# A selective-scan unit and the end of a pair: half a projection, gelu and silu are reordered, and VectorE takes over three steps at the end

## The chip, the cores and the metric

The kernel runs on one core of a Trainium2 chip. The metric is the device time of one execution in microseconds. The engines are named as in the profile: PE (TensorE, with PEld for its weight loads), DVE (VectorE), ACT (ScalarE), POOL (GpSimd) and SP (SyncE, which issues most DMAs). Each engine runs its own list of instructions in order and waits on semaphores.

## The reference, cut to what matters

Two blocks are computed on 16 images of 48 channels and 64x64 pixels: a depthwise 3x3 conv with a routed expert (gelu, then a 1x1 "point" conv), an FFN, a frequency-domain Mamba block on four quadrants, and a second FFN. The part that the change touches is the Mamba block and the conv that runs beside it:

```python
xz = jnp.einsum('blc,ec->ble', xs, in_w)
xi, z = (xz[..., :d_inner], xz[..., d_inner:])
# 4-tap causal conv along the sequence, then
xi = jax.nn.silu(...)
delta = jax.nn.softplus(jnp.einsum('blr,dr->bld', dt, dt_w) + dt_b)
dA = jnp.exp(delta[..., None] * A)
dBu = delta[..., None] * Bm[:, :, None, :] * xi[..., None]
h = dA_t * h + dBu_t            # along the sequence of 1024
y = einsum('bds,bs->bd', h, C_t) + xi * Dp
out = einsum('bld,cd->blc', y * jax.nn.silu(z), out_w)
```

## The kernel before

The 16 images go through in 8 pairs (p). In each pair the Mamba block has 4 quadrants times 2 images, that is 8 units (v = 0 to 7), and each unit has 12 groups or slots (m = 0 to 11) of 128 rows (8 channels times 16 states) by 1024 positions. All engines walk the same written order, `scan_stage`: for every unit and slot the engine's `early(m, v+1)`, `step(v, m)`, `conv(m, v)` and `prep(m, v+1)`, in this order, each of which does something only in its own slots. So while unit v is scanned, the next unit is prepared and one eighth of the next pair's expert conv is computed. The last pair has no conv beside it.

One slot, in the lines of the profile:

- SP (`spread_delta`) copies 8 rows of delta to 128 rows by a DMA of 512 KB (arena<-dl). There are three buffers, and the DMA for group n waits until the decay of group n-3 is made.
- ACT (`decay`, L1224) makes exp(delta*A) of the group two slots ahead. It needs the DMA and a free one of three result buffers.
- PE (`broadcast_u`, L834 and L836) spreads u into two PSUM banks, one slot ahead.
- DVE multiplies it in PSUM by B (L1558) and scans (L1563).
- POOL multiplies the states by C (L1649, `product`).
- PE (`states`, L853) sums three products into y, in PSUM banks 0 and 1, in slots 4, 7 and 10 and in slot 1 of the next unit (or at the very end, for unit 7).

The next unit's preparation runs in fixed slots. PE projects the first half of xi (`project_in`, L740) in slot 11 of the unit before the one that prepares it, and the second half in slot 0. ACT makes silu of xi (L1120) in slot 1, after `step` of that slot and so behind its decay, silu of z (L1130) in slot 3, softplus and a copy of B and C (L1142, L1155) in slot 4. Each of these has a table load in front (L1209, L1180, L1136) and the exp table behind it (L977). PE's products for z (L747) and for delta, B and C (L753) stand between them. Also in slot 2 ACT copies y out of PSUM (`copy_y`, L1248), and POOL gates it with silu of z (`gate`, L1658); the next silu of z waits for that gate.

The conv: nine taps on PE (L912, slots 5 to 9), gelu on ACT (L1279, slot 10, behind that slot's decay), the point product on PE (L918, slot 11, waits for gelu), its bias on ACT (`mix_bias`, L1268, slot 0, in front of that slot's decay). The second half of xi's projection shares a PSUM bank with the conv and waits for the bias.

The end of a pair: after the last scan come POOL's last product, PE's last `states`, ACT's copy of y, POOL's gate, PE's output projection (L862, two halves), ACT's two copies out (L1238) and PE's transposes (L658) with which the inverse transform goes on. `keep_warm` (L759) gives PE four matmuls without use beside the last `states`.

## Time and profile before

| | |
|---|---|
| device time, median of 3 runs | 4347.82 us (4341.52 to 4351.54) |
| the profiled execution's own time | 4323.44 us |
| its span, first to last instruction | 4321.6 us |
| busy share of the span | PE 87%, DVE 80%, ACT 65%, POOL 55% |
| mean granted TensorE clock | 0.949 of full speed |
| chain that ended last, by engine | DVE 30%, PE 23%, issue 21%, ACT 14%, DMA 7%, POOL 5% |

The span covers the eight pairs one behind the other; about two thirds of a pair is the scan stage. The busy shares are averages over stages with different limits, so the rows further down are taken from single stages.

### The profile page before, as it was taken

How to read it: one execution, taken by the hardware profiler on the slowest of the kernel's cores; microseconds unless marked ns; L12 is line 12 of the kernel's file. 1: busy time of each engine (PE TensorE's matmuls, PEld its weight loads, DVE VectorE, ACT ScalarE, POOL GpSimd, SP SyncE). 2: the span in 40 equal slices, each digit the busy share in tenths (PEclk: the TensorE clock that was granted, in tenths of full speed). 3: DMA queues.
4: the chain of work that ended last, by engine and by line, in shares of the span. 5: the costliest groups of instructions: out<-in, count | busy, mean ns of one | idle time of the engine just before them, and what ended most of it. 6: DMA issues, size and time to landing. Idle time of an engine off the chain costs nothing.

```text
span 4321.6 us, 41656 instructions
## 1 busy us (share of the span) xinstructions
PE 3774.4 (87%) x13976; PEld 1368.9 (32%) x13976; DVE 3470.1 (80%) x3077; ACT 2792.2 (65%) x3228; POOL 2380.3 (55%) x1108
## 2 busy tenths in 40 slices
PE   6889988899879998899988999889988899878887
PEld 2332234222342223422234222432234322342223
DVE  1479977799778996699966998679976799778996
ACT  2566757677566775676666775767756677576754
POOL 0147762577426873177732787237762487525773
PEclk9999999999999999999999999999998999998878
DMA  1168861787518883288824886258861588607881
GB/s 39 45 142 206 208 153 46 182 205 197 127 55 205 205 210 88 75 203 210 202 69 108 220 205 161 75 149 204 218 152 47 142 222 199 146 15 190 196 202 44
DMA packets 186044, 644.71 MB, mean 149 GB/s; under 512 B 25660, under 2 KB 26600, under 8 KB 182280
## 3 DMA queue, kind: packets, MB, share of 16 engines
q1 hardware_dynamic: 168808, 596.95, 56.7%
q10 hardware_dynamic: 17024, 45.10, 3.5%
q8 instruction: 113, 1.85, 0.2%
q14 instruction: 99, 0.81, 0.1%
HBM read 525.40 MB, written 78.82 MB: 140 GB/s over the span
## 4 chain that ended last, share of the span: by engine, by line
DVE 30%; PE 23%; issue 21%; ACT 14%; DMA 7%; POOL 5%; SPq 0%; DVEq 0%; ACTq 0%; POOLq 0%
DVE arena L1563 12%; DVE ps L1558 11%; DMA arena<-dl 6%; PE ps L667 4%; PE ps L607 3%; PE ps L834 2%; POOL arena L1658 2%; PE ps L658 2%; POOL arena L1649 2%; ACT arena L1020 2%; ACT arena L1224 2%; ACT arena L1002 2%; PE ps L853 2%; PE ps L686 1%; PE ps L740 1%
## 5 line engine op out<-in xcount | busy, mean ns | idle before, releaser
L1649 POOL TENSOR_TENSOR arena<-arena 128x1024 f32<-128x1024 f32 x768 | 1804.4, 2358 | 737.6 <-DVE arena L1563 737.6
L1563 DVE TENSOR_TENSOR_SCAN arena<-arena,ps 128x1024 f32<-128x1024 f32 x768 | 1756.4, 2287 | 75.2 <-issue 35.7
L1224 ACT ACTIVATE arena<-arena,a_all 128x1024 f32<-128x1024 f32 x768 | 869.4, 1146 | 798.1 <-DMA arena<-dl 656.1
L1558 DVE TENSOR_TENSOR ps<-ps,arena 128x1024 f32<-128x1024 f32 x768 | 929.5, 1210 | 116.1 <-PE ps L836 115.6
L834 PE MATMUL ps<-arena,spread 32*128 32x512 f32 x1536 | 890.9, 661 | 137.3 <-DVE arena L1563 136.3
L836 PE MATMUL ps<-arena,spread 32*128 32x512 f32 x1536 | 883.7, 663 | 0.0
L853 PE MATMUL ps<-arena,gather 128*32 128x512 f32 x3072 | 533.1, 643 | 18.8 <-POOL arena L1649 18.8
L912 PE MATMUL ps<-x 96*96 96x512 f32 x1008 | 500.3, 614 | 23.8 <-ACT arena L1155 23.8
L834 PEld LDWEIGHTS ps<-arena,spread 32*128 32x128 f32 x1536 | 232.8, 188 | 779.1 <-DVE arena L1563 411.9
L1608 POOL TENSOR_TENSOR x<-x,arena 96x512 f32<-96x512 f32 x64 | 113.3, 1771 | 373.0 <-DVE arena L1402 373.0
L977 ACT ACT_TABLE_LOAD x226 | 290.0, 1283 | 24.7 <-DMA wo<-in_wo 20.6
L740 PE MATMUL ps<-arena,w_in 96*96 96x512 f32 x512 | 258.3, 634 | 0.1
L912 PEld LDWEIGHTS ps<-x 96*96 96x96 f32 x1008 | 142.9, 163 | 348.5 <-issue 348.5
L607 PE MATMUL ps<-arena,average 96*96 96x512 f32 x400 | 226.3, 649 | 29.9 <-ACT arena L1013 29.6
L853 PEld LDWEIGHTS ps<-arena,gather 128*32 128x32 f32 x3072 | 106.5, 114 | 403.9 <-issue 300.8
L1002 ACT ACTIVATE arena<-ps,eps 96x512 f32<-96x512 f32 x200 | 136.8, 684 | 148.5 <-PE ps L607 148.2
L836 PEld LDWEIGHTS ps<-arena,spread 32*128 32x128 f32 x1536 | 229.5, 188 | 0.0
L1658 POOL TENSOR_TENSOR arena<-arena 96x1024 f32<-96x1024 f32 x64 | 150.5, 2352 | 134.3 <-ACT arena L1248 134.3
L1627 POOL MEMSET arena<- 96x6 f32 x8 | 0.8, 103 | 399.5 <-DVE xq L1525 399.5
L1371 DVE TENSOR_TENSOR arena<-ps,arena 96x512 fp8e5<-96x512 f32 x128 | 86.9, 679 | 129.3 <-ACT arena L1007 129.1
L1020 ACT ACTIVATE arena<-ps 128x1536 f16<-128x1536 f32 x128 | 183.8, 1436 | 1.7 <-PE ps L626 1.6
L1608 POOL TENSOR_TENSOR x<-col_all,arena 96x512 f32<-96x512 f32 x64 | 104.3, 1629 | 144.4 <-DVE arena L1402 144.4
(157 smaller groups left out, 4896.1 us busy)
## 6 DMA issues: line engine op xcount, KB each, us to landing
arena<-dl SPq DMA_DIRECT2D x880, 512.0 KB, 6.9
dl<-arena ACTq DMA_DIRECT2D x64, 384.0 KB, 5.7
x<-pn SPq DMA_DIRECT2D x56, 247.5 KB, 10.2
arena<-in_x SPq DMA_DIRECT2D x9, 1536.0 KB, 16.2
arena<-xq SPq DMA_DIRECT2D x64, 192.0 KB, 6.1
arena<-arena ACTq DMA_DIRECT2D x64, 192.0 KB, 7.5
out<-x SPq DMA_DIRECT2D x64, 192.0 KB, 2.1
arena<-xq SPq DMA_DIRECT2D x64, 191.8 KB, 5.4
```

The lines of the kernel that those rows point to most:

```text
L607: pe.matmul(ps[0:R, LN_DEPTH + j % LN_DEPTH, :], average[:], sq[:, j % LN_DEPTH, :], start=True, stop=True).then_inc(averaged, 1)
L740: mm = pe.matmul(ps[0:DI, 6 + c, :], w_in[:, q, j, :], xs[:, i, c * 512 + 2 * j:c * 512 + 2 * j + 512], start=(j == 0), stop=(j == 1))
L834: pe.matmul(ps[:, bank, :], spread[rows[0], r, :], u[rows[0], i, 0:512], start=True, stop=True)
L836: pe.matmul(ps[:, bank + 1, :], spread[rows[1], r, :], u_low[rows[1], i, :], start=True, stop=True).then_inc(ubc_ready, 1)
L853: mm = pe.matmul(ps[b * BLK:(b + 1) * BLK, c, :], gather[:, r, :], hs[:, (r * TRIO + b) % HSS, c * 512:(c + 1) * 512], start=False, stop=( ...
L912: mm = pe.matmul(ps[0:R, 7, :], diag[:, k, :], taps_of(win[:, v % 2], k), start=(k == 0), stop=(k == TAPS - 1), skip_group_check=True)
L977: exp_table = lambda: act.preload_act_table_set("natural_log_exp_and_others")
L1020: act.activation(hf[:, j % 2, :], ps[:, 4:7, :].rearrange("p b n -> p (b n)"), ACT.Copy).then_inc(hf_ready, 1)
L1224: act.activation(da[:, m % DAS, :], dbc[:, m % DBC, :], ACT.Exp, scale=a_all[:, v // 2, m:m + 1]).then_inc(da_ready, 1)
L1558: dve.tensor_tensor(driven, driven, bmat[:, v % 2, :], ALU.mult).then_inc(bu_ready, 1)
L1563: dve.tensor_tensor_scan(hs[:, m % HSS, :], da[:, m % DAS, :], driven, 0.0, ALU.mult, ALU.add).then_inc(h_ready, 1)
L1649: pool.tensor_tensor(product, product, cmat[:, v % 2, :], ALU.mult).then_inc(pr_ready, 1)
```

## The change

Four things are moved or rewritten.

1. PE: the first half of xi's projection for the unit after next (slot 11) is issued in front of the point product instead of behind it (`half_ahead`).
2. ACT: gelu is issued in front of slot 10's decay instead of behind it, and silu of xi in front of slot 1's decay instead of behind it.
3. The end of a pair: DVE makes the last product, the gate (straight from PSUM, so that no copy of y is made) and the second half of the copy out. POOL and ACT no longer do these.
4. `keep_warm` at the end of a pair has three matmuls instead of four, and one more stands in each of slots 0, 2 and 4 of unit 7.

```diff
-WARM_XI, WARM_SCAN, WARM_GATE = 4, 2, 4
+WARM_XI, WARM_SCAN, WARM_GATE = 4, 2, 3
+WARM_LAST = {0: 1, 2: 1, 4: 1}
...
-                    if slot == PE_XI_EARLY and v + 1 < UNITS:
-                        pe.wait_ge(xs_in[1 - i], (p * QUADS + (v + 1) // 2 + 1) * XSL)
-                        pe.wait_ge(bc_ready, bc_count(p, v))
-                        if v >= 3 and i == 1:
-                            pe.wait_ge(mo_copied, 2 * (p * QUADS + (v - 1) // 2))
-                        project_in(V + 1, (v + 1) // 2, 1 - i, 0)
...
                 def states(v, r):
-                    pe.wait_ge(pr_ready, (p * UNITS + v) * G + TRIO * (r + 1))
+                    if v == UNITS - 1 and r == GPB - 1:
+                        pe.wait_ge(last_pr, p + 1)
+                        pe.wait_ge(pr_ready, pr_count(p, v, G - 1))
+                    else:
+                        pe.wait_ge(pr_ready, pr_count(p, v, TRIO * (r + 1)))
...
+                def half_ahead(v):
+                    q, i = divmod(v + 2, 2)
+                    pe.wait_ge(xs_in[i], (p * QUADS + q + 1) * XSL)
+                    pe.wait_ge(bc_ready, bc_count(p, v + 1))
+                    if v >= 2 and i == 0:
+                        pe.wait_ge(mo_copied, 2 * (p * QUADS + v // 2))
+                    project_in(p * UNITS + v + 2, q, i, 0)
...
                 def conv(slot, v):
                     if v == UNITS - 1:
                         invert_early(slot)
+                        keep_warm(WARM_LAST.get(slot, 0))
+                    if slot == PE_XI_EARLY and v + 2 < UNITS:
+                        half_ahead(v)
...
                 def early(slot, v):
+                    if slot == ACT_SILU and v >= 2:
+                        act.preload_act_table(ACT.Silu)
+                        silu_xi(v)
+                        exp_table()
...
                 def prep(slot, v):
-                    if slot == ACT_SILU and v >= 2:
-                        act.preload_act_table(ACT.Silu)
-                        silu_xi(v)
-                        exp_table()
...
                 def step(v, m):
+                    if m == ACT_GELU and not last:
+                        gelu(v)
...
                 def final():
-                    copy_y(UNITS - 1)
...
-                    copy_out(QUADS - 1, 1, 7)
...
+                def final():
+                    dve.wait_ge(h_ready, n + 1)
+                    dve.tensor_tensor(hs[:, slot, :], hs[:, slot, :], cmat[:, i, :],
+                                      ALU.mult).then_inc(last_pr, 1)
+                    dve.wait_ge(y_acc, (V + 1) * GPB)
+                    dve.wait_ge(sz_ready, 2 * V + 2)
+                    dve.wait_ge(mo_ready, 2 * (p * QUADS + q))
+                    dve.tensor_tensor(yz[:, i, :], two(0, DI), sz[:, i, :], ALU.mult).then_inc(yz_ready, 1)
+                    dve.wait_ge(mo_ready, 2 * (p * QUADS + q) + 2)
+                    dve.tensor_copy(colq[:, q // 2, q % 2][:, QH // 2:QH, :],
+                                    ps[:, 7, :].rearrange("p (h w) -> p h w", w=QH)).then_inc(mo_copied, 1)
...
                 def step(v, m):
+                    if v < UNITS - 1 or m < G - 1:
+                        pool.tensor_tensor(product, product, cmat[:, v % 2, :],
+                                           ALU.mult).then_inc(pr_ready, 1)
...
                 def final():
-                    gate(UNITS - 1)
```

The order of instructions on ACT around the border of two units, from the decay of the next unit's group 0 to copy_y, before. L1224 is a decay, L1275 and L1279 are gelu's table and gelu, L977 is the exp table, L1268 the conv's bias, L1209 and L1120 silu's table and silu of xi, L1248 copy_y.

```order
L1224 ACTIVATE arena<-arena,a_all 128x1024 x3
L1275 ACT_TABLE_LOAD
L1279 ACTIVATE arena<-ps,sel_small 96x512
L977 ACT_TABLE_LOAD
L1224 ACTIVATE arena<-arena,a_all 128x1024
L1268 ACTIVATE x<-ps,pw_bias 96x512
L1224 ACTIVATE arena<-arena,a_all 128x1024 x2
L1209 ACT_TABLE_LOAD
L1120 ACTIVATE arena<-ps,small_all 96x512 x2
L977 ACT_TABLE_LOAD
L1248 ACTIVATE arena<-ps 96x1024
```

The same place on ACT in the changed kernel, where the lines have moved: L1240 is a decay, L1290 and L1294 are gelu, L993 the exp table, L1286 the bias, L1196 and L1136 silu of xi, L1264 copy_y.

```order
L1240 ACTIVATE arena<-arena,a_all 128x1024 x2
L1290 ACT_TABLE_LOAD
L1294 ACTIVATE arena<-ps,sel_small 96x512
L993 ACT_TABLE_LOAD
L1240 ACTIVATE arena<-arena,a_all 128x1024 x2
L1286 ACTIVATE x<-ps,pw_bias 96x512
L1240 ACTIVATE arena<-arena,a_all 128x1024
L1196 ACT_TABLE_LOAD
L1136 ACTIVATE arena<-ps,small_all 96x512 x2
L993 ACT_TABLE_LOAD
L1240 ACTIVATE arena<-arena,a_all 128x1024
L1264 ACTIVATE arena<-ps 96x1024
```

One decay (group 0) has moved from ahead of gelu to behind it, and one (group 3) from ahead of silu of xi to behind it.

PE in slots 10 and 11 of the unit before, and in slot 0: L834 and L836 are a broadcast, L918 is the point product, L740 a half of xi's projection.

```order
L834 MATMUL ps<-arena,spread 128x512
L836 MATMUL ps<-arena,spread 128x512
L918 MATMUL ps<-arena,pw_gated 96x512
L740 MATMUL ps<-arena,w_in 96x512 x2
L834 MATMUL ps<-arena,spread 128x512
L836 MATMUL ps<-arena,spread 128x512
L740 MATMUL ps<-arena,w_in 96x512 x2
```

The same place on PE in the changed kernel (L934 is the point product, L746 a half of the projection).

```order
L834 MATMUL ps<-arena,spread 128x512
L836 MATMUL ps<-arena,spread 128x512
L746 MATMUL ps<-arena,w_in 96x512 x2
L934 MATMUL ps<-arena,pw_gated 96x512
L834 MATMUL ps<-arena,spread 128x512
L836 MATMUL ps<-arena,spread 128x512
L746 MATMUL ps<-arena,w_in 96x512 x2
```

The first half of the projection and the point product have changed places.

DVE at the end of a pair, before: the last multiply (L1558) and scan (L1563), then the additions of the inverse transform (L1546) and its copies (L1473).

```order
L1558 TENSOR_TENSOR ps<-ps,arena 128x1024
L1563 SCALAR_TENSOR_TENSOR arena<-arena,ps 128x1024
L1546 TENSOR_TENSOR xd<-xd,ps 128x384 x4
L1473 COPY xq<-ps 96x8x64 x2
L1579 TENSOR_TENSOR x<-x,ps 96x512 x8
```

DVE at the end of a pair in the changed kernel (L1571, L1576, L1559 and L1486 are the lines that were L1558, L1563, L1546 and L1473).

```order
L1571 TENSOR_TENSOR ps<-ps,arena 128x1024
L1576 SCALAR_TENSOR_TENSOR arena<-arena,ps 128x1024
L1587 TENSOR_TENSOR arena<-arena 128x1024
L1592 TENSOR_TENSOR arena<-ps,arena 96x1024
L1595 COPY col_all<-ps 128x16x32
L1559 TENSOR_TENSOR xd<-xd,ps 128x384 x4
L1486 COPY xq<-ps 96x8x64 x2
```

Three rows have come in between the last scan and the additions: the last product, the gate and the second half of the copy out.

## Rows read from the trace of the kernel before

**Rows 1.** Stretches: length, busy PE, PEld, DVE, ACT, POOL, clock, DMA share, GB/s.

```profile
2414.61:2630.08 215.47, 200.44 (x700) 55.79 (x696) 204.99 (x121) 156.80 (x155) 169.78 (x76) 1.00 0.85 212
...
3974.75:4186.16 211.41, 179.22 (x600) 46.32 (x598) 205.10 (x120) 137.73 (x135) 163.82 (x71) 0.84 0.84 199
sum 1750.35, PE 1617.93 PEld 446.14 DVE 1642.39 ACT 1236.50 POOL 1353.09; mean PE 202.24 PEld 55.77 DVE 205.30 ACT 154.56 POOL 169.14
```

**Rows 2.** The page's costliest groups: busy us, mean ns, idle before it and releasers.

```profile
L1563 DVE TENSOR_TENSOR_SCAN arena<-arena,ps 128x1024 f32<-128x1024 f32 x768 | 1756.4, 2287 | 75.2 <-issue 35.7
...
L1558 DVE TENSOR_TENSOR ps<-ps,arena 128x1024 f32<-128x1024 f32 x768 | 929.5, 1210 | 116.1 <-PE ps L836 115.6
```

**Rows 3.** Timeline, pair 4, unit 2: start, length, instruction, idle before and releaser.

```profile
2437.99 1.15 ACT L1224 ACTIVATE arena<-arena,a_all 128x1024 f32<-128x1024 f32 x1 [2.29 <-DMA arena<-dl]
...
2440.19 1.15 ACT L1224 ACTIVATE arena<-arena,a_all 128x1024 f32<-128x1024 f32 x1 [1.05 <-DMA arena<-dl]
...
2441.36 1.28 ACT L1209 ACT_TABLE_LOAD   x1
...
2445.22 1.02 ACT L1248 ACTIVATE arena<-ps 96x1024 f32<-96x1024 f32 x1
...
2457.18 3.23 ACT L1224 ACTIVATE arena<-arena,a_all 128x1024 f32<-128x1024 f32 x3
...
2458.41 2.29 DVE L1563 TENSOR_TENSOR_SCAN arena<-arena,ps 128x1024 f32<-128x1024 f32 x1 [1.29 <-issue]
```

**Rows 4.** Busy time by stretch, pair 4, units 2 and 3.

```profile
2458.30:2480.60 22.30, 22.30 (x81) 6.02 (x78) 21.98 (x13) 13.58 (x15) 17.29 (x8) 1.00 1.01 263
2439.10:2458.30 19.20, 16.48 (x61) 4.67 (x60) 16.79 (x10) 17.82 (x20) 15.30 (x8) 1.00 0.69 164
```

**Rows 5.** Timeline of ACT: the first and the last of 48 decays of group 3.

```profile
309.25 1.15 ACT L1224 ACTIVATE arena<-arena,a_all 128x1024 f32<-128x1024 f32 x1 [1.04 <-DMA arena<-dl]
...
4167.90 1.15 ACT L1224 ACTIVATE arena<-arena,a_all 128x1024 f32<-128x1024 f32 x1 [1.11 <-DMA arena<-dl]
```

**Rows 6.** Timeline, pair 4, unit 1, slots 10 and 11.

```profile
2429.51 1.15 ACT L1224 ACTIVATE arena<-arena,a_all 128x1024 f32<-128x1024 f32 x1 [4.16 <-DMA arena<-dl]
...
2431.97 0.68 ACT L1279 ACTIVATE arena<-ps,sel_small 96x512 f32<-96x512 f32 x1
...
2433.65 1.88 PE L740 MATMUL ps<-arena,w_in 96*96 96x512 f32 x4
```

**Rows 7.** Three smaller groups by line, same columns as rows 2.

```profile
L759 PE MATMUL ps<-spread,gather 128*32 128x512 f32 x160 | 78.9, 635 | 11.3 <-DVE xq L1525 11.3
...
L918 PE MATMUL ps<-arena,pw_gated 96*96 96x512 f32 x112 | 62.1, 637 | 22.5 <-ACT arena L1279 22.5
...
L1538 DVE TENSOR_TENSOR arena<-arena 96x1024 f32<-96x1024 f32 x8 | 9.8, 1221 | 85.4 <-ACT arena L1142 85.4
```

**Rows 8.** Busy time by stretch: a stretch at the lower clock, pair 1, unit 4.

```profile
958.10:971.70 13.60, 13.60 (x28) 3.03 (x26) 9.55 (x6) 7.69 (x8) 6.59 (x3) 0.50 0.76 178
```

**Rows 9.** Timeline: the end of pair 4.

```profile
2691.54 2.37 POOL L1649 TENSOR_TENSOR arena<-arena 128x1024 f32<-128x1024 f32 x1 [1.09 <-DVE arena L1563]
...
2694.98 2.34 POOL L1649 TENSOR_TENSOR arena<-arena 128x1024 f32<-128x1024 f32 x1 [1.08 <-DVE arena L1563]
2697.38 0.63 PE L853 MATMUL ps<-arena,gather 128*32 128x512 f32 x3 [2.06 <-POOL arena L1649]
...
2699.35 1.02 ACT L1248 ACTIVATE arena<-ps 96x1024 f32<-96x1024 f32 x1 [6.12 <-PE ps L853]
...
2700.45 2.34 POOL L1658 TENSOR_TENSOR arena<-arena 96x1024 f32<-96x1024 f32 x1 [3.13 <-ACT arena L1248]
...
2702.85 1.94 PE L862 MATMUL ps<-arena,wo 96*64 96x512 f32 x8 [1.80 <-POOL arena L1658]
2703.97 1.91 ACT L1238 ACTIVATE col_all<-ps 128x512 f32<-128x512 f32 x2 [2.10 <-PE ps L862]
```

**Rows 10.** Busy time by stretch, sum of eight: last scan's end to the transposes.

```profile
sum 92.58, PE 53.30 PEld 12.55 DVE 0.00 ACT 34.83 POOL 46.26; mean PE 6.66 PEld 1.57 DVE 0.00 ACT 4.35 POOL 5.78
```

More of the change, by code:

```diff
@@ L404, in scan_stage, with pr_count @@
             last()
+        def pr_count(p, v, m):
+            return p * (UNITS * G - 1) + v * G + m
         def bc_count(p, v):
@@ L1268, in mix_bias, with gelu @@
                     act.activation(pwb, ps[0:R, 7, :], ACT.Identity, bias=pw_bias[:, 0:1]).then_inc(pwb_ready, 1)
[L1270 to L1281 removed]
+                def gelu(v):
+                    act.preload_act_table(ACT.Gelu)
+                    act.wait_ge(taps_ps, (p + 1) * NCH + v + 1)
+                    if v:
+                        act.wait_ge(pw_ps, (p + 1) * NCH + v)
+                    act.activation(gel, ps[0:R, 7, :], ACT.Gelu,
+                                   bias=sel_small[:, TAPS:TAPS + 1]).then_inc(gelu_ready, 1)
+                    exp_table()
                 def final():
[L1284 removed]
                     if not last:
@@ L1288, in final @@
                     copy_out(QUADS - 1, 0, 6)
-                    copy_out(QUADS - 1, 1, 7)
-                scan_stage(prep, first, step, conv, final, early)
+                scan_stage(prep, first, step, lambda slot, v: None, final, early)
                 evac_turned(p, xq, inverted, evens(NG // 2, NG), INV_BANK)
```

36 lines of the change are left out of this document (14 added, 22 removed).

## The prediction

> **What bounds the kernel now.** I read the stretches first. [rows 1] cut the scan stages: each stretch runs from the scan of group 6 in unit 1 to the same scan in unit 6, five units, and the sum is over all eight pairs. The 40 units take 1750.35 us, 43.76 each, and DVE is busy for 1642.39 of them, 41.06 each. DVE is the engine nearest to its limit, but something stops it for up to 2.7 us in each unit, 108 us in all. [rows 2] name it: 115.6 us before the multiply, ended by PE's broadcast, and 35.7 before the scan with "issue", where DVE waits for nothing that the profile names.
>
> The timeline of one unit shows what is late [rows 3]. The scan of group 6 starts at 2458.41, 1.29 late, and the decay that it needs is the first of the three that begin at 2457.18: it ends at 2458.33, so the "issue" wait is ACT. Going back from there ACT works almost without a pause to 2439.14, the end of group 2's decay: a wait of 1.05 for a DMA, group 3's decay, silu of xi with two tables (2441.36 to 2445.22), copy_y, and then the decays, silu of z and softplus that the program puts there. This chain is 19.2 us long. The broadcast that stops the multiply a step earlier hangs on the same chain: it stands on PE behind the products that wait for silu of z.
>
> What starts the chain is the landing of group 2's DMA. [rows 4] show the two halves of a cycle. From group 6's decay until the next unit's group 2 has landed (2458.3 to 2480.6) the DMA engines are full: share 1.01, 263 GB/s. While ACT's chain runs (2439.1 to 2458.3) they stand at 0.69 and 164 GB/s, and ACT is busy for 17.82 of 19.2. Full DMA, then full ACT: 22.3, a decay of 1.15 and about 19 make 42.5 a unit, which is more than DVE's 41.06. This cycle is what the scan stage runs at.
>
> Outside the scan the place to read is the end of a pair [rows 9]. From POOL's last product (2694.98) to the projection (2702.85) one engine works at a time: POOL 2.34, PE 1.95, ACT 1.02, POOL 2.34, with hops between. In the eight stretches from the last scan's end to the transposes DVE is busy for 0.00 of 92.58 us [rows 10].
>
> **Silu of xi in front of group 3's decay.** ACT now begins silu's table at the end of group 2's decay, and group 3's DMA lands while silu runs. The decay's 1.15 stays in the chain; the wait in front of it goes. That wait was 1.05 here, 1.04 in the first and 1.11 in the last of 48 places [rows 3, 5]; over the 48 its mean is 0.93. Silu also needs the second half of the projection. Taking at each of the 42 places of the first seven pairs the later of the two gives a mean of 0.87. Since the DMA half of the cycle starts at group 6's decay, it moves with the chain, and the 0.87 counts in every unit: 42 x 0.87 = 36.5 us. The DVE limit is not reached (43.1 a unit in pair 4, 41.0 busy [rows 1]). The last pair has only 211.41 - 205.10 = 6.3 to give, some of it gaps between instructions, and there the half projection comes late more often: 2.5. Sum 39; the bounds are 0, if the DMA half grows by as much, and 54 (48 x 1.05 plus a part of the PE waits). I take the upper side, because in [rows 4] the DMA engines have room exactly where group 3 is now late. What is late next: group 3's decay ends 2.8 us later than before (3.86 + 1.15 after group 2's, for 1.05 + 1.15), and DMA 6 is issued that much later. Scan 3 stands about three steps of 3.44 before the 2457.1 at which scan 6 could have gone, so it keeps 1 to 2 us, and DMA 6 lands into the slack part.
>
> **Gelu in front of group 0's decay.** ACT waits 4.16 for that decay's DMA [rows 6]; gelu's block is two tables of 1.28 and 0.68, 3.24, and fits. Where the taps end late it does not, and the decay comes up to 2.3 late; it is used some 5 us later. On ACT nothing is gained or lost: 0. If that cover were gone, 2.3 in half of 42 units, 48 us, would be the cost.
>
> **Half projection in front of the point product.** PE waited 22.5 us in all for gelu at the point product [rows 7]. The half projection (1.88 [rows 6]) now fills that time. Where there was no wait, the point product comes 1.88 later, and with it the bias on ACT, behind which group 2's decay is queued. That decay waits for its DMA anyway (2.29 [rows 3]), which covers it: 0. The PE time itself is no gain, but what follows the wait is: [rows 8] is a stretch of 13.6 us at a granted clock of 0.50, that is 1.2 GHz, right behind such a wait; DVE is busy for 9.55 in it, against 0.95 of the time in pair 4, where the clock is 1.00 [rows 1]. That is 3.4 lost. Three units (pairs 0, 1 and 3) have their chain lengthened so, by about 3 us each. I take 9 us, with bounds of -5 (it falls elsewhere) and +20.
>
> **The end of a pair.** Removed: POOL's product 2.34, copy_y 1.02, POOL's gate 2.34, and five hops of about 0.04 to 0.1 that become four: 7.87 from 2694.98, plus 0.07 before it [rows 9]. New: DVE's product at 1.22 (the nearest row with both inputs in SBUF, L1538 [rows 7]), PE's 1.95, DVE's gate from PSUM at 1.21 (L1558 [rows 2]), hops 0.1: 4.5. Gain 3.4. The three keep_warm matmuls end before that: eight rows of L759 at 0.49 [rows 7] become six. The second copy out now runs beside ACT's first, but it can start only when the projection ends at 2704.79, and ACT's pair was done at 2705.88: between 0 and 0.9, taken as 0 because a copy takes about 1 us. 8 x 3.4 = 27; bounds 18 (product at POOL's 2.34) and 34.
>
> **keep_warm in unit 7.** Three more a pair, 2 x 0.49 each, 24 us of PE. PE has no silu products to wait for in unit 7, so slots 0 and 2 are free; the one in slot 4 stands in front of taps and transforms that fill PE. It costs up to 1 a pair, and a clock that stays up gives as much back: 0, bounds -8 and +8.
>
> **Sum.** 39 + 9 + 27 = 75 us. Against the profiled execution 4323.4 - 75 = 4248. The runs shown have a median 24.4 above that execution, and the change leaves what makes that difference alone: 4347.8 - 75 = 4273 us. A change of less than 0.2% (8.7 us) can't be told from none here.
>
> **Rivals.**
> A second case is that only the end of a pair counts: the DMA half starts earlier but takes as long as it must, since the total of bytes a unit is the same, and DVE waits as before. For it speaks a DMA share of 0.85 over whole stretches [rows 1]; against it the 0.69 [rows 4]. 4347.8 - 27 = 4321.
> A third: PE's clock falls in more places, for instance in slot 3, where PE then waits for silu of z. At 3 us each, ten more of them and none saved: 4273 + 9 + 30 = 4312.
> On the other side: the point product, 1.88 later, makes the bias end after group 2's DMA has landed. From there on each microsecond delays group 2's decay and the whole chain. It decides when the bias ends later than the landing; of the 2.29 in [rows 3] the 1.88 leave 0.4. If all 42 units lost the 1.88, the scan stages would lose 42 x (1.88 - 0.87) = 42, less 27 at the ends: 4362, slower.
> A fifth: DVE's product cannot run beside POOL. If POOL still worked at the scan's end, DVE would wait up to 2.34 in each pair: 4273 + 19 = 4292. But POOL's product of group 10 ends at 2693.91, 1.0 before the last scan does, and so in all eight pairs [rows 9].
> The Trainium skill, page "SBUF — State Buffer", section "Who interferes with whom", states just this: a DVE instruction with two inputs in SBUF and a GpSimd one that reads SBUF lock each other out for the whole instruction. By that rule the new product is the first DVE instruction of the scan stage that could be held up, and the page would agree with the fifth case only if POOL were late; no run here shows such an overlap.
> A sixth: with PE no longer late the waits go further down, to DVE's limit: 108 of [rows 1] less some 12 of gaps, and 27: 4225 to 4240.
>
> **Chances.** The forecast 0.62, with a range of its own of 4255 to 4292; only the ends 0.15; more slow stretches 0.08; the bias late, slower, 0.05; POOL in the way 0.04; down to DVE's limit 0.06. The range 4240 to 4322 leaves out the slower case and the outer halves of the second and the sixth. Faster by over 0.2%: 0.92; within: 0.03; slower: 0.05.
>
> **What would show it.** In the trace after: group 3's decay without a wait, and group 6's decay 18.2 after group 2's; a mean unit near 42.8; POOL's columns of the end gone and about 7.7 from the last scan's end to the transposes; no wait of PE for gelu at the point product; fewer stretches at 0.50 at the start of a unit. The prediction is wrong if the stretch from group 6's decay to the landing of group 2 grows, if the bias on ACT waits for PE, or if DVE waits for PE at scan 3 or 5 as long as before.

## The result and the profile after

The changed kernel takes 4223.67 us (median of four runs, 4219.27 to 4236.07); the kernel before, beside it, 4344.67 (4333.06 to 4351.54). The ratio is 0.9729, with a 95% interval of 0.9699 to 0.9759: 118 us less by the ratio, 121 by the medians. The forecast was 75 less and a lowest end of 4240. The direction was right; the time lies below the range.

The profiled execution took 4219.27 us, 104 less than the one before (4323.44), at a mean granted clock of 0.967 instead of 0.949. It lies 4 us below its runs' median; the one before lay 24 below.

Stretches of the changed kernel from the scan of group 6 in unit 1 to the same scan in unit 6, cut and laid out as [rows 1]: pair 4, the last pair, the sum of eight.

```profile
2355.80:2568.98 213.18, 200.42 (x698) 55.80 (x696) 204.88 (x120) 156.34 (x155) 169.45 (x76) 1.00 0.87 213
...
3877.50:4085.62 208.12, 178.38 (x600) 46.35 (x598) 204.89 (x120) 137.43 (x135) 163.69 (x71) 0.84 0.84 202
sum 1701.78, PE 1584.70 PEld 437.74 DVE 1639.73 ACT 1234.25 POOL 1352.81; mean PE 198.09 PEld 54.72 DVE 204.97 ACT 154.28 POOL 169.10
```

The sum is 48.6 us lower and DVE's busy time the same within 3: nearly all of it is waiting that went. A unit takes 1701.78 / 40 = 42.54, where 42.8 was foreseen. PE's busy time fell by 33 for the same matmuls, most of it by a higher clock. The page's costliest groups (as [rows 2]) say which wait went:

```profile
L1576 DVE TENSOR_TENSOR_SCAN arena<-arena,ps 128x1024 f32<-128x1024 f32 x768 | 1756.4, 2287 | 74.6 <-issue 31.6
...
L1571 DVE TENSOR_TENSOR ps<-ps,arena 128x1024 f32<-128x1024 f32 x768 | 928.3, 1209 | 57.5 <-PE ps L836 57.2
```

DVE's wait for PE's broadcast halved (115.6 before); the wait behind group 6's decay is nearly as it was. The same unit as in [rows 3], in the timeline of the changed kernel:

```profile
2378.50 1.15 ACT L1240 ACTIVATE arena<-arena,a_all 128x1024 f32<-128x1024 f32 x1 [1.88 <-DMA arena<-dl]
...
2379.66 1.28 ACT L1196 ACT_TABLE_LOAD   x1
...
2383.53 1.15 ACT L1240 ACTIVATE arena<-arena,a_all 128x1024 f32<-128x1024 f32 x1
...
2396.52 3.23 ACT L1240 ACTIVATE arena<-arena,a_all 128x1024 f32<-128x1024 f32 x3
...
2397.76 2.29 DVE L1576 TENSOR_TENSOR_SCAN arena<-arena,ps 128x1024 f32<-128x1024 f32 x1 [0.64 <-DVE ps L1571]
```

Silu's table (L1196) starts 0.01 after group 2's decay, group 3's decay (2383.53) has no wait, and group 6's decay ends at 2397.67: 18.02 after group 2's, where it was 19.19. Over units 1 to 6 of the first seven pairs the mean of this chain went from 19.31 to 18.05; the time from group 6's decay to the next unit's group 2 stayed (24.62 and 24.65, 35 places). The 24.62 holds units that were slowed by half clock: in the cycles without any, this half grew by 0.3 (24.29 and 24.58). The cycle still ends at group 6.

The end of pair 4 (as [rows 9]), and the sum of the eight stretches from the last scan's end to the transposes (as [rows 10]):

```profile
2631.74 1.22 DVE L1587 TENSOR_TENSOR arena<-arena 128x1024 f32<-128x1024 f32 x1
...
2632.24 1.86 POOL L1697 TENSOR_TENSOR x<-x 96x512 f32<-96x512 f32 x1 [1.54 <-ACT x L1286]
2633.02 0.63 PE L857 MATMUL ps<-arena,gather 128*32 128x512 f32 x3 [1.64 <-DVE arena L1587]
...
2634.99 1.22 DVE L1592 TENSOR_TENSOR arena<-ps,arena 96x1024 f32<-96x1024 f32 x1 [2.03 <-PE ps L857]
...
2636.27 1.94 PE L866 MATMUL ps<-arena,wo 96*64 96x512 f32 x8 [0.44 <-DVE arena L1592]
...
2638.25 1.01 DVE L1595 COPY col_all<-ps 128x512 f32<-128x512 f32 x1 [2.04 <-PE ps L866]
```

```profile
sum 63.19, PE 40.48 PEld 10.16 DVE 27.69 ACT 18.40 POOL 11.99; mean PE 5.06 PEld 1.27 DVE 3.46 ACT 2.30 POOL 1.50
```

From the last scan's end, 2631.70, to the transposes, 2639.41, it takes 7.71; the eight sum to 63.19, 29.4 less than before. The row of POOL is the conv's last addition (`mix`); it starts while DVE's product (L1587) runs.

Between the two profiled executions the 104 us lie as follows. Units 0 to 6 of the first seven pairs make 52 of them (2138.8 and 2086.6), unit 7 of these pairs 9, the scan stage of the last pair 3, and all that stands outside the scans 40. Of the 40, 29 are the ends of the pairs, and 16 are one stage between pairs 5 and 6 that ran at half clock for 44.4 us before and does not in the changed kernel (last section). In all, the granted clock stood at half for 438 us before and for 274 after.

### The profile page after: what moved, and what is told of

Read it like the earlier page. It is cut to its first block, busy times and chain, and to the rows that moved or that the text cites. A ratio compares the mean times of both kernels' runs of the same rounds, so it can differ in the third digit from the quotient of the medians.

```text
span 4217.4 us, 41720 instructions
## 1 busy us (share of the span) xinstructions
PE 3708.7 (88%) x14008; PEld 1348.4 (32%) x14008; DVE 3493.2 (83%) x3101; ACT 2772.9 (66%) x3212; POOL 2345.8 (56%) x1092
## 4 chain that ended last, share of the span: by engine, by line
DVE 35%; issue 25%; PE 18%; ACT 13%; DMA 4%; POOL 4%; SPq 0%; DVEq 0%; ACTq 0%; POOLq 0%
DVE ps L1571 15%; DVE arena L1576 13%; PE ps L673 4%; DMA arena<-dl 3%; PE ps L613 3%; PE ps L664 2%; ACT arena L1036 2%; ACT arena L1018 2%; POOL arena L1689 2%; POOL arena L1680 2%; ACT arena L1240 2%; PE ps L692 2%; DVE arena L1424 1%; ACT L1152 1%; ACT arena L1029 1%
## 5 line engine op out<-in xcount | busy, mean ns | idle before, releaser
L1680 POOL TENSOR_TENSOR arena<-arena 128x1024 f32<-128x1024 f32 x760 | 1785.9, 2359 | 704.3 <-DVE arena L1576 704.3
L1576 DVE TENSOR_TENSOR_SCAN arena<-arena,ps 128x1024 f32<-128x1024 f32 x768 | 1756.4, 2287 | 74.6 <-issue 31.6
L1240 ACT ACTIVATE arena<-arena,a_all 128x1024 f32<-128x1024 f32 x768 | 869.8, 1146 | 692.1 <-DMA arena<-dl 541.4
L834 PE MATMUL ps<-arena,spread 32*128 32x512 f32 x1536 | 876.4, 652 | 142.7 <-DVE arena L1576 140.9
L1571 DVE TENSOR_TENSOR ps<-ps,arena 128x1024 f32<-128x1024 f32 x768 | 928.3, 1209 | 57.5 <-PE ps L836 57.2
L836 PE MATMUL ps<-arena,spread 32*128 32x512 f32 x1536 | 869.1, 653 | 0.0
L857 PE MATMUL ps<-arena,gather 128*32 128x512 f32 x3072 | 519.4, 629 | 12.5 <-DVE arena L1587 12.4
L834 PEld LDWEIGHTS ps<-arena,spread 32*128 32x128 f32 x1536 | 230.1, 186 | 785.9 <-DVE arena L1576 482.8
L746 PE MATMUL ps<-arena,w_in 96*96 96x512 f32 x512 | 246.6, 609 | 8.0 <-ACT x L1286 7.8
L857 PEld LDWEIGHTS ps<-arena,gather 128*32 128x32 f32 x3072 | 104.9, 112 | 384.8 <-issue 299.3
L836 PEld LDWEIGHTS ps<-arena,spread 32*128 32x128 f32 x1536 | 226.7, 186 | 0.0
L643 PE MATMUL ps<-arena,w 128*96 128x512 fp8e5 x384 | 105.4, 384 | 83.4 <-DVE arena L1376 77.6
```

Of the source, the lines that this page charges most:

```text
L746: mm = pe.matmul(ps[0:DI, 6 + c, :], w_in[:, q, j, :], xs[:, i, c * 512 + 2 * j:c * 512 + 2 * j + 512], start=(j == 0), stop=(j == 1))
L834: pe.matmul(ps[:, bank, :], spread[rows[0], r, :], u[rows[0], i, 0:512], start=True, stop=True)
L836: pe.matmul(ps[:, bank + 1, :], spread[rows[1], r, :], u_low[rows[1], i, :], start=True, stop=True).then_inc(ubc_ready, 1)
L857: mm = pe.matmul(ps[b * BLK:(b + 1) * BLK, c, :], gather[:, r, :], hs[:, (r * TRIO + b) % HSS, c * 512:(c + 1) * 512], start=False, stop=( ...
L1240: act.activation(da[:, m % DAS, :], dbc[:, m % DBC, :], ACT.Exp, scale=a_all[:, v // 2, m:m + 1]).then_inc(da_ready, 1)
L1571: dve.tensor_tensor(driven, driven, bmat[:, v % 2, :], ALU.mult).then_inc(bu_ready, 1)
```

## The experiments

Each kernel was compared with the kernel before on the same chip; us is (1 - ratio) x 4340. A part that is "moved" is the part of the diff shown above, alone. The intervals are some 9 to 19 us wide to either side, so differences of 20 us between two rows are at the edge of what the ratios can tell; where the text decides more finely, it goes by the traces, of which there is one for each kernel.

| kernel | ratio, 95% interval | us less | mean clock of its runs |
|---|---|---|---|
| before, again | 0.9999 (0.9969 to 1.0029) | 0 | 0.946 |
| silu of xi moved | 0.9892 (0.9847 to 0.9936) | 47 | 0.948 |
| half projection and gelu moved | 0.9983 (0.9952 to 1.0014) | 7 | 0.945 |
| end of a pair | 0.9939 (0.9907 to 0.9971) | 26 | 0.946 |
| keep_warm in unit 7 | 0.9992 (0.9970 to 1.0013) | 3 | 0.950 |
| silu, half projection and gelu | 0.9844 (0.9813 to 0.9876) | 68 | 0.960 |
| silu and gelu | 0.9845 (0.9807 to 0.9882) | 67 | 0.956 |
| silu and half projection | 0.9824 (0.9785 to 0.9862) | 76 | 0.958 |
| silu and one keep_warm in slot 11 | 0.9834 (0.9803 to 0.9864) | 72 | 0.959 |
| all but keep_warm in unit 7 | 0.9788 (0.9751 to 0.9825) | 92 | 0.960 |
| the whole change | 0.9729 (0.9699 to 0.9759) | 118 | 0.966 |

**The parts alone.** First the kernel before as a control, then three parts.

> The kernel before, unchanged, run again: a control for the step of the forecast that took the runs' offset of 24 us over the profiled execution as a constant. Theory 1 (the offset is something around the execution that stays): every execution here lies near 4345 us whatever its granted clock. Theory 2 (the offset is TensorE's clock, and the profiled execution of before was a lucky one): time and mean granted clock go together. From the two profiles 0.949 goes with 4323 us; a stretch at half clock of 13.6 us cost 3.4, a quarter, so 0.01 less clock (some 86 us more at half clock) should cost some 20 us: executions at 4345 us should show 0.935 to 0.942.

Theory 2 held in the main, with a higher clock than foreseen: executions at 4344 to 4347 us show 0.944 or 0.945. Twelve executions of one program took 4319.85 to 4363.46 us, the fastest at a clock of 0.950, the slowest at 0.940; of 28 executions of before beside them the fastest (4311.23) had 0.956. Over these 40 a fitted line loses 28 us for 0.01 of clock and accounts for some 70% of the spread. The profiled execution of before stood near the fast end.

```
-   (ACT, prep of slot 1, behind group 3's decay)  table Silu; silu_xi(v); exp_table()
+   (ACT, early of slot 1, in front of it)         table Silu; silu_xi(v); exp_table()
```

> Only silu of xi moves in front of group 3's decay. Theory 1 (the forecast's term for this edit is right, and the excess lies elsewhere): 36 to 46 us faster than before (42 units of 0.87 to 1.03, and up to 3 in the last pair), the stretches at half clock inside the scan stages remain, some 120 us of them in the first seven pairs. Theory 2 (the shorter chain on ACT is also what keeps TensorE's clock up): 65 us faster or more, and few stretches at half clock left in the scan stages. Rival (the DMA half of the cycle grows by as much): within 10 us of before.

47 us, with an interval of 28 to 66: theory 1, a little above its upper end. The traces put it lower, within the same interval. From group 2's decay to the next unit's, in units 1 to 5 of the first seven pairs, the cycles without any half clock take 43.33 and 43.27 on average in the two profiles of before (23 and 24 of 35 cycles) and 42.53 here (23): 0.77 a unit, some 32 us over 42 units, with an uncertainty of some 18.

```
-   (ACT, POOL)  copy_y(UNITS - 1); gate(UNITS - 1); copy_out(QUADS - 1, 1, 7); last product on POOL
+   (DVE)        last product; gate from PSUM; half of the copy out       WARM_GATE 4 -> 3
```

> Only the end of a pair changes: DVE makes the last product, the gate and half of the copy out, three keep_warm matmuls in place of four. Theory 1: 24 to 28 us faster (3.1 to 3.4 in each of eight pairs), nothing else moves. Theory 2 (the end also changes TensorE's clock in the stage behind it, as the 44 us stretch in pair 5 of before): 35 us or more.

26 us, with an interval of 13 to 40: theory 1 by its size. But the 44 us stretch that theory 2 speaks of is missing in this kernel's one profile, where the stage between pairs 5 and 6 takes 164.1 against 184.1 in the control: 3.4 of the 20 are the end. How often it is missing was not measured, and the ratio can't tell 27 from 27 and 16 more.

```
-   (PE)   project_in(V + 1, ..., 0) in prep of slot 11, behind the point product
+   (PE)   half_ahead(v) in conv of slot 11, in front of it
-   (ACT)  gelu in conv of slot 10      + (ACT)  gelu(v) in step of slot 10, in front of the decay
```

> Only the half projection and gelu move. Theory 1 (the forecast: they are worth the few stretches at half clock behind the wait for gelu): 0 to 10 us faster. Theory 2 (they are where the excess comes from, since they fill TensorE's wait at the border of units): 30 to 50 us faster, mean granted clock up by 0.015 or more, and nearly no stretch at half clock in slots 0 to 4 of a unit of the first seven pairs. Rival (nothing but a later bias): 0 or slower.

7 us and no more clock: theory 1 in size, but not for its reason. The stretches at half clock had not gone, they had moved: in units 0 to 6 of the first seven pairs silu alone has 95.6 us at half clock, all in slots 11 and 0, and this kernel 105.8, all but 6.8 in slots 2 and 3. The kernel before has both kinds, 54.6 and 27.3. PE's groups by line say why (columns as [rows 7]): with silu alone moved, with half projection and gelu alone, and with all three.

```profile
L747 PE MATMUL ps<-arena,w_in 96*96 96x512 f32 x256 | 124.7, 609 | 0.0
L918 PE MATMUL ps<-arena,pw_gated 96*96 96x512 f32 x112 | 63.7, 651 | 23.1 <-ACT arena L1279 22.8
```

```profile
L747 PE MATMUL ps<-arena,w_in 96*96 96x512 f32 x256 | 136.1, 657 | 29.2 <-ACT arena L1125 29.1
L923 PE MATMUL ps<-arena,pw_gated 96*96 96x512 f32 x112 | 57.7, 596 | 0.0
```

```profile
L747 PE MATMUL ps<-arena,w_in 96*96 96x512 f32 x256 | 124.7, 609 | 0.1
L923 PE MATMUL ps<-arena,pw_gated 96*96 96x512 f32 x112 | 57.7, 596 | 0.0
```

PE has two holes at the border of a unit: the point product's wait for gelu (slot 11; L918 and L923), and z's wait for silu of xi (slot 2, L747). Each edit closes one. With silu alone the first is open, and the timeline (pair 4, unit 2) shows what it costs:

```profile
2409.43 0.68 ACT L1279 ACTIVATE arena<-ps,sel_small 96x512 f32<-96x512 f32 x1
...
2410.17 1.10 PE L918 MATMUL ps<-arena,pw_gated 96*96 96x512 f32 x2 [1.73 <-ACT arena L1279]
...
2413.76 1.21 PE L834 MATMUL ps<-arena,spread 32*128 32x512 f32 x1
...
2415.89 1.23 DVE L1558 TENSOR_TENSOR ps<-ps,arena 128x1024 f32<-128x1024 f32 x1 [1.83 <-PE ps L836]
```

PE waits 1.73, its clock falls to the lower level, the broadcast takes 1.21 instead of 0.69, and DVE waits. With half projection and gelu alone the second hole opens instead, and the half clock falls on PE's products that ACT waits for (pair 6, unit 4):

```profile
3587.37 3.43 PE L753 MATMUL ps<-arena,w_dbc 96*128 96x512 f32 x4
...
3590.84 0.68 ACT L1147 ACTIVATE arena<-ps,small_all 96x512 f32<-96x512 f32 x1 [0.75 <-PE ps L753]
...
3591.90 1.23 DVE L1562 TENSOR_TENSOR ps<-ps,arena 128x1024 f32<-128x1024 f32 x1 [4.16 <-PE ps L830]
```

**The two holes together.**

> Silu of xi, gelu and the half projection move; the end of a pair and unit 7 stay as before. Alone, silu was worth 40 to 47 us and half projection with gelu 7, with the mean granted clock at 0.945 to 0.949 in each; in the first the stretches at half clock stand in slot 0 of a unit, in the second in slots 2 and 3. Theory 1 (the parts add): 47 to 54 us faster than before, clock 0.948. Theory 2 (TensorE has two holes at the border of a unit, the wait for gelu and the wait for silu of xi; each edit closes one, and the clock stays up only when both are closed): 65 to 85 us faster, mean clock 0.953 to 0.958, nearly no stretch at half clock left in slots 0 to 4 of units 1 to 6 in the first seven pairs, those in unit 7 as before.

68 us, with 47 + 7 apart, and the clock at 0.960: theory 2. Units 0 to 6 of the first seven pairs, busy time by stretch, make it plain (columns as [rows 1]). First the kernel with silu alone, which shows the price of the clock inside one execution: pair 4 at 0.94 and pair 5 at 1.00 differ by 12.5 us, and the DVE work is the same within 1.2.

```profile
2326.34:2635.89 309.55, 294.46 (x962) 81.02 (x960) 288.09 (x169) 218.02 (x215) 231.87 (x102) 0.94 0.85 207
2848.72:3145.78 297.06, 279.00 (x962) 77.48 (x960) 286.93 (x169) 217.36 (x215) 231.97 (x102) 1.00 0.88 215
...
sum 2123.02, PE 1997.73 PEld 551.50 DVE 2011.68 ACT 1523.87 POOL 1623.62; mean PE 285.39 PEld 78.79 DVE 287.38 ACT 217.70 POOL 231.95
```

The same sum of the kernel before (the control's profile), with half projection and gelu alone, and with all three:

```profile
sum 2133.86, PE 1986.04 PEld 548.67 DVE 2011.78 ACT 1527.20 POOL 1623.74; mean PE 283.72 PEld 78.38 DVE 287.40 ACT 218.17 POOL 231.96
```

```profile
sum 2145.46, PE 2004.53 PEld 555.22 DVE 2011.59 ACT 1531.06 POOL 1624.12; mean PE 286.36 PEld 79.32 DVE 287.37 ACT 218.72 POOL 232.02
```

```profile
sum 2080.86, PE 1954.57 PEld 541.98 DVE 2008.52 ACT 1521.35 POOL 1623.49; mean PE 279.22 PEld 77.43 DVE 286.93 ACT 217.34 POOL 231.93
```

In these executions silu alone gives 11, half projection and gelu alone lose 12, and together they give 53. The 12 is within the spread of one program: the same units, unchanged, take 2133.9 to 2162.2 in four profiles (before, the control, and the kernels with the end of a pair or unit 7 alone changed).

Is it the hole, or the order of the matmuls? Two kernels close it by one of the two edits:

> Silu of xi and gelu moved; the half projection stays behind the point product. Theory 2 (what counts is that TensorE has no hole in slot 11, whoever closes it): gelu comes earlier and the wait for it is gone, so clock 0.957 or more and 65 to 80 us faster than before, as with all three moved. Theory 3 (what counts is the order on TensorE: with the half projection still behind the point product, two matmuls more stand between gelu and the broadcast of group 1): 40 to 55 us faster, DVE still waits at group 1 of units 2, 4 and 6.

> Silu of xi and the half projection moved; gelu stays behind group 0's decay. Theory 2: the half projection (some 1 us) fills the wait for gelu of up to 1.7 and leaves less than 1 us of hole: clock 0.957 or more, 65 to 80 us faster. Theory 3: the same time, since the order on TensorE is the same. If gelu's place is what counts, 40 to 55 us faster and the clock at 0.948.

67 and 76 us, alike within their intervals: either will do, and theory 3 falls (DVE's waits at group 1 of units 1 to 6 are zero in the first of them). Their intervals overlap that of silu alone; what parts them from it is the clock in the profiles. In units 0 to 6 of the first seven pairs these two and the one with all three moved have 0 or 6.8 us at half clock and take 2080.9 to 2086.9. The six with a hole open (before, the control and the four with one part changed) have 64.9 to 139.9 and take 2123.0 or more. Two more fill the holes with matmuls whose result nobody uses:

```
     if slot == PE_PW:
+        keep_warm(3)
         pe.wait_ge(gelu_ready, ...)
```

> Silu of xi moved, and three keep_warm matmuls (some 1.5 us, they compute nothing that is used) in front of TensorE's wait for gelu in slot 11; half projection and gelu stay where they were. Theory 2 (the clock falls because TensorE has a hole at this place; any work that fills it keeps the clock up): mean clock 0.955 to 0.960 as with the half projection moved, 65 to 80 us faster than before, hardly a stretch at half clock in slots 0 and 11 of units 1 to 6. Rival (the moved half projection helps because what follows it comes sooner, not because the hole is filled): clock 0.948, 40 to 47 us faster as with silu alone, or less by the added work.

```
     if slot == PE_Z (v >= 2):
+        keep_warm(3)
```

> Half projection and gelu moved, and three keep_warm matmuls in front of TensorE's wait for silu of xi in slot 2 (units 2 on); silu stays where it was. Theory 2: the stretches at half clock in slots 2 and 3 of units 1 to 6 go, clock 0.953 to 0.958, and by the clock alone 25 to 45 us faster than before, where half projection and gelu alone gave 4 to 7. Rival (the hole is not what the clock goes by, or the added matmuls delay the broadcasts): within 10 us of before, clock 0.947 or less.

Both brought units 0 to 6 to a clock of 1.00 and were worth little in time: 0.9916 and 0.9990. I had sized the filler wrongly: a keep_warm shows as two matmul records of some 0.45, so three took 2.7 over a hole of 1.7, and DVE waited 0.93 or 1.90 at group 1 of most units of the first. That is not all of it: its units 0 to 6 take 2101.01, 22 less than with silu alone, and what it loses again stands in unit 7, where the filler also stands (318.3 against 308.3), and outside the scans (1541.7 against 1529.6). Why was not followed up. In the second the units 0 to 6 of seven pairs came down from 2145.46 to 2125.20, but the last pair, whose PE has no conv, lost as much to the filler (its scan stage took 359.6 instead of 340.0), and DVE still waited 83 us at groups 5 and 6 of units 1 to 6 of all pairs (97 without the filler): ACT's chain is as long as before (mean 19.05), and the clock helps little where that is late. With a filler shorter than the hole in slot 11:

> Silu of xi moved, and one keep_warm matmul in front of TensorE's wait for gelu, in place of three. The profile of the run with three shows that each is two passes of 0.45 to 0.49, so the three took 2.7 to 2.9 us over a hole of some 1.7, and DVE waited 0.93 or 1.90 at group 1 of every unit. One takes 0.9 and leaves less than 1 us of hole. Theory 2 (any work that fills the hole will do): no wait at group 1, no stretch at half clock in units 0 to 6, clock 0.956, 60 to 75 us faster than before, as with the half projection in the hole. Rival (the half projection itself has to be out of the way): 40 to 50 us faster, as with silu alone.

72 us: one matmul that computes nothing, 0.9 us in slot 11, does what moving half projection and gelu does. The sum of units 0 to 6 is between silu alone and all three:

```profile
sum 2096.45, PE 1993.30 PEld 548.74 DVE 2010.51 ACT 1522.47 POOL 1623.64; mean PE 284.76 PEld 78.39 DVE 287.22 ACT 217.50 POOL 231.95
```

**Unit 7.**

```
+WARM_LAST = {0: 1, 2: 1, 4: 1}     keep_warm(WARM_LAST.get(slot, 0)) in unit 7
```

> Only the three keep_warm matmuls in unit 7 are added. Theory 1 (the forecast's term): within 8 us of before. Theory 2 (they keep the clock up in unit 7, where before has 54 us at half clock in the first seven pairs): the stretches of unit 7 go, clock up by 0.003 to 0.006, and at some 28 us per 0.01 of clock 8 to 17 us faster.

> The changed kernel without the three keep_warm matmuls in unit 7. Theory 1 (they are worth nothing): within 8 us of the changed kernel, so 110 to 125 us faster than before. Theory 2 (they carry a part of the excess): stretches at half clock come back in slots 1 to 5 of unit 7, 40 us or more of them in the first seven pairs, clock 0.960 or less, 100 to 108 us faster than before.

Alone 3 us and undecided. Taken out of the change, 26 by the two ratios (92 and 118); the intervals overlap. The traces give less: unit 7 of the first seven pairs takes 303.7 in the change and 308.7 without them, 304.2 with them alone and 312.4 and 316.4 in the two profiles of before. So in unit 7 itself they are worth 5 to 12. In the one profile without it half clock in unit 7 is back (44.4 us there in the first seven pairs, 13.7 with it), and a stretch of 44.4 us between pairs 0 and 1, told of below, makes up 14.6 of the 27 between the two profiles. Another 10.6 lie in units 0 to 6, where the two programs are the same.

**Does ACT's chain still set the pace?** Six kernels try to beat the change. The copy of B and C, 1.02 us of the chain, goes behind group 6's decay:

```
 (ACT, early of slot 4)  softplus(v)
-                        keep_bc(v)
 (ACT, prep of slot 4)   delta_to_rows(v)
+                        keep_bc(v)
                         bc_to_rows(v)
```

> The changed kernel with the copy of B and C moved behind group 6's decay, so that ACT's chain from group 2 to group 6 is 1.02 us shorter again. Theory 1 (full DMA, then ACT's chain is still the cycle): 15 to 40 us faster than the changed kernel, group 6's decay some 17 us after group 2's. Theory 2 (after the change DVE or PE is the limit): within 8 us of it. On the other side: B and C reach PE's taps and the DMAs 1.1 later, PE gets a new hole in slot 5, and it is 5 to 20 slower than the changed kernel.

The other side came, far stronger than foreseen: ratio 1.0483, 4530 us, clock 0.894. The timeline (pair 4, unit 2) shows a third hole:

```profile
2594.47 2.82 PE L928 MATMUL ps<-x 96*96 96x512 f32 x4 [2.35 <-ACT arena L1171]
...
2597.22 1.21 PE L834 MATMUL ps<-arena,spread 32*128 32x512 f32 x1
...
2599.34 1.23 DVE L1571 TENSOR_TENSOR ps<-ps,arena 128x1024 f32<-128x1024 f32 x1 [2.19 <-PE ps L836]
```

PE waits 2.35 for the copy, then works at half clock for 14 to 17 us, in nearly every unit, and DVE waits 392.7 us in all for its broadcasts. So the hole was filled, and the taps spread in other ways (the expectations take four keep_warm for 2.0 us; in the trace they are eight records and took 3.6):

```
+WARM_TAPS = 4      keep_warm(WARM_TAPS) in front of the taps' wait in slot 5
```

> The changed kernel with the copy of B and C behind group 6's decay, as in the run that was 300 us slower than the changed kernel and showed a hole of 2.35 us on TensorE in front of the conv's taps in slot 5 and half clock behind it in most units; now with four keep_warm matmuls (2.0 us) in front of that wait. Theory 2 (all of the loss was the clock behind the hole): the stretches in slot 6 go, and the time is that of the changed kernel or up to 40 us less. Rival (the later copy of B and C costs by itself): still 50 us or more slower than the changed kernel, at a clock of 0.96.

```
-CONV_TAPS = {5: (0, 1), 6: (2, 3), 7: (4,), 8: (5, 6), 9: (7, 8)}
+CONV_TAPS = {6: (0, 1), 7: (2, 3), 8: (4, 5), 9: (6, 7, 8)}
```

> As the run before it, but the conv's taps begin in slot 6 instead of 5, so that the wait for the copy of B and C does not stand in front of the broadcasts of slot 5; the four keep_warm matmuls stay in slot 5. Theory 2: as the run before or 5 to 15 us less, and faster than the changed kernel. Rival (taps packed into four slots delay the broadcasts of slots 8 and 9, gelu comes later): 10 to 30 us slower than the changed kernel.

```
+CONV_TAPS = {6: (0, 1, 2), 7: (3, 4), 8: (5, 6), 9: (7, 8)}      WARM_TAPS = 2
```

> The changed kernel with the copy of B and C behind group 6's decay, the conv's taps from slot 6 on, three of them in slot 6 and two in each of 7 to 9, and two keep_warm matmuls in slot 5. With three taps in slot 9 DVE had waited 1.24 at group 9 in every even unit and some 0.7 in odd ones, and no longer at group 6. If that place alone took the gain back: 5 to 25 us faster than the changed kernel. If TensorE is full from slot 6 to 9 wherever the third tap stands: 20 to 50 us slower than the changed kernel, with the wait at group 7 or 8.

```
+CONV_TAPS = {6: (0, 1), 7: (2, 3), 8: (4, 5), 9: (6, 7), 10: (8,)}      WARM_TAPS = 2
```

> As the run before, but two taps in each of slots 6 to 9 and the last one in slot 10, so that gelu waits for it in front of group 0's decay. If TensorE's room in slots 6 to 9 is what was missing: 5 to 25 us faster than the changed kernel. If gelu's lateness costs (it ends behind the landing of group 0's DMA, and the point product waits for it): a hole in slot 11, half clock behind it, and 10 to 50 us slower than the changed kernel.

```
-WARM_TAPS = 4      +WARM_TAPS = 2      (taps from slot 5, as in the first of these)
```

> The changed kernel with the copy of B and C behind group 6's decay and two keep_warm matmuls in slot 5 (1.8 us for a hole of 2.35) in place of four, which took 3.6 and so kept the taps 1.3 us behind the copy that they wait for. If the overfull slot was the 1.51 that DVE waited at group 7 of every unit: no such wait, and 5 to 25 us faster than the changed kernel, 120 to 145 faster than before. If the taps are late by the copy itself: a wait of 0.5 or more at group 7, and the time of the changed kernel or slower.

Ratios 0.9916, 0.9853, 0.9784, 0.9827 and 0.9792: none beats the change's 0.9729, and each came out as the slower of the cases foreseen for it, the second slower still (54 us behind the change, where 10 to 30 stood). The half clock that was expected with the last tap in slot 10 did not come in units 0 to 6. In the last one the clock is 1.00 in units 0 to 6, the chain's mean is 17.05 and DVE's wait at group 6 is gone, but the other half of the cycle grew from 24.65 to 25.8, and DVE waits 0.7 (odd units) and 1.0 (even) on average at group 7 and 0.4 at groups 8 to 10 of even units, for broadcasts that stand on PE behind taps, keep_warm and the projection out. So in the changed kernel ACT's chain is still what is late, but with the taps in these slots shortening it gains nothing: PE's room comes right behind it.

With the last tap in slot 10 it does gain. Units 0 to 6 of that kernel, and of the change:

```profile
sum 2064.78, PE 2027.21 PEld 559.86 DVE 2011.10 ACT 1501.78 POOL 1623.47; mean PE 289.60 PEld 79.98 DVE 287.30 ACT 214.54 POOL 231.92
```

```profile
sum 2086.60, PE 1957.74 PEld 542.15 DVE 2008.72 ACT 1524.82 POOL 1624.38; mean PE 279.68 PEld 77.45 DVE 286.96 ACT 217.83 POOL 232.05
```

The 22 us are lost again in unit 7 (326.2 against 303.7), and 43 more outside the scans (1533.2 against 1489.8), where the stages behind a pair are 3 to 6 longer and one, between pairs 0 and 1, 17. A kernel with these taps in units 0 to 6 alone was not built. How much of the 24.65 is DMA and how much PE was not separated.

## Why the prediction was wrong

**The term that failed is the 9 us for PE's clock**, in the part on the half projection, together with "three units" as its extent. The mechanism was right, half clock behind a wait of PE, but not its size. The trace of before had it: in units 1 to 5 of the first seven pairs all 35 cycles take 43.99 on average, the 23 without half clock 43.33. That is 0.66 a unit, and some 28 us over 42 units (0.59 and 25 in the control). The prediction counted three stretches of 13.7 us, 41 of the 81.9 us at half clock in units 0 to 6, and left out the 27.3 that stand in slots 2 and 3, where PE waits for silu of xi. With silu moved, closing the hole in slot 11 was worth 20 to 29 us in four kernels (67 to 76 against 47, with some 20 of uncertainty); half projection and gelu without it gave 7. The prediction read one stretch [rows 8] and three units, and added the edits up. They don't add: while silu of xi is late, PE's clock falls there instead (next to the place that the third rival names, but behind silu of xi, not silu of z, and in the edit taken alone), and while gelu is late, at the other place. The parts alone sum to 47 + 7 + 26 + 3 = 83, near the forecast 75; the whole is 118, and the missing 35 have some 30 of uncertainty. 13 to 22 of them are the two holes (67 to 76 against 47 + 7); the rest lies within the intervals.

**The offset of 24 us did not stay.** "The change leaves what makes that difference alone" was wrong: a part of the difference was TensorE's clock, which varies from execution to execution, and the change takes away many of the places where it falls. By the control's line 0.949 against 0.946 makes some 10 of the 24; the rest is spread that the clock does not explain. That is 17 of the 46 us by which the forecast missed: the two profiles differ by 104, the medians by 121. Of the other 29 (104 - 75), 16 are the stage between pairs 5 and 6, which no term of the prediction touches and whose cause stays open; 9 are unit 7 and 7 are units 0 to 6. In all three it is stretches at half clock that have gone.

**Silu in front of group 3's decay: right.** 39 foreseen, 47 measured (interval 28 to 66), and by the traces some 32 in 42 units and 2 to 3 in the last pair. Group 3's decay has no wait, the chain is 1.08 shorter in the median unit (19.10 and 18.02), where 0.87 was the mean wait. The other half of the cycle grew by a quarter of that in the cycles without half clock (from 24.29 and 24.23 to 24.51 with silu alone), not by as much, so the second rival falls, for this step.

**The end of a pair: right.** 27 foreseen, 26 measured, 29 by the stretches; 7.71 from scan to transposes, where 7.7 was written. The fifth rival did not come: POOL's own products end before the last scan does. But DVE and POOL do meet, the other way round. In five of the eight pairs the conv's last addition on POOL (L1697, shown above) starts 0.5 us after DVE's product. The product takes 1.22 in all eight; the addition takes 1.84 to 1.86 in these five and 1.25 to 1.29 in its other 51 places, and ends 1.1 after the product. So POOL waited and DVE did not, and the next step of the chain, PE's sums (L857), went on without it. The Trainium skill, page "SBUF — State Buffer", section "Who interferes with whom", says that of two such instructions the order of issue decides which one is blocked. The trace agrees with that.

**Gelu at nothing, the bias covered: right.** Moved with the half projection they cost no wait that shows, and the slower rival (the bias behind the point product) did not come, though its sign did: the bias, which waited for PE once before, by 0.1, now waits in 19 of 49 places between two units, 16.6 us in all. Group 2's wait for its DMA covers that in 46 of the 49; in three the decay follows the bias at once.

**keep_warm in unit 7 at nothing: too low.** The ratios leave it undecided, 3 alone and 26 in the whole, by overlapping intervals; the traces show 5 to 12 in unit 7.

**The sixth rival, down to DVE's limit**, had the time (4225 to 4240) but not the mechanism: 62 us of DVE's waits are left in the five-unit stretches (1701.78 - 1639.73). Of these 16 are gaps of under 0.1 between two instructions, 35 stand at group 6 and 8 at group 5. Before, 34 stood at group 6, 33 at group 5 and 21 at groups 1 to 3: the first of these stayed, and most of the others went.

## What to carry to other kernels

Two edits that each remove a cause of the same loss are not to be added: ask what the loss does when only one cause is gone, and price the pair. Before costing a wait of PE by its length, look at the granted clock in the stretch behind it, and at whose chain the slowed matmuls stand in. When runs of one program differ by 1%, set time against clock before taking an offset as fixed. Where a loss hits some units and not others, the units that it misses price every other term, from one trace.

## What the runs showed of the hardware

- The price of a hole is not in the hole: a wait of 1.73 or 2.35 us on PE was followed by 14 to 17 us at 1.2 GHz, and it showed in the time where DVE or ACT's chain stood behind it. In the last pair, without the conv, the clock is 0.84 in the changed kernel and a unit is still faster (208.12 for five against 213.18).
- One matmul of no use, in a wait, was worth as much as a reordering: 72 against 68 us. Three of them there kept the clock up as well and gave 36 in all, less than silu alone with its 47, by overlapping intervals.
- A product on DVE with both inputs in SBUF and an addition on POOL that overlapped it did not run side by side: DVE's took 1.22 as ever, POOL's 1.84 to 1.86 in place of 1.25 to 1.29.
- Between pairs 5 and 6 both profiles of before (the control too) show 44.4 us at a granted clock of 0.50, right behind a wait of 2.35 of PE in the feed-forward stage; the stage is 16 to 18 us longer there. Seven more kernels with the old end show it too (41.0 in one), and two that fill the hole in slot 11 don't. With the new end alone it is missing; in three kernels with the new end it stood between pairs 0 and 1 instead, and in the changed kernel nowhere. Each was profiled once. What places it stays open.

```profile
3305.98 1.05 PE L637 MATMUL ps<-arena,w 128*96 128x512 fp8e5 x3 [2.35 <-DVE arena L1363]
```

```profile
3306.40:3350.80 44.40, 39.04 (x118) 26.36 (x117) 20.91 (x42) 19.70 (x38) 2.30 (x2) 0.50 0.23 73
```
